# Weights of rounds 2 and 3 of an expert network read from a ring of three places that on-chip copies fill

## The reference

```python
cur = xn
for r in range(4):                      # R = 4 rounds
    logits = cur @ Wg[r] + bg[r]        # E = 4 experts
    vals, idx = top_k(logits, 2)
    cw = sum(one_hot(idx, 4) * softmax(vals))
    hmid = gelu(einsum('nh,ehf->enf', cur, W1) + b1)    # 128 -> 512, all four experts
    y = einsum('enf,efh->enh', hmid, W2) + b2           # 512 -> 128
    cur = cur + einsum('ne,enh->nh', cw, y)
```

## Time and profile before

| | us |
|---|---|
| median of 2 runs | 784.92 (784.88 to 784.97) |
| span of the profiled execution, first to last instruction | 782.9 |
| TensorE with matmuls in flight | 777.2 |
| VectorE busy | 689.3 |
| ScalarE busy | 641.1 |
| POOL busy | 115.2 |

### The profile page before, as it was taken

The page is one execution under the profiler, slowest core; times in us unless marked ns, Lnnn a source line. Parts: engine busy times, 40 slices in busy tenths (PEclk is TensorE's granted clock), DMA queues, the critical chain, the costliest instruction groups (busy, mean ns, idle before and its releaser), DMA issues.

```text
span 782.9 us, 9951 instructions
## 1 busy us (share of the span) xinstructions
PE 777.2 (99%) x3392; PEld 619.2 (79%) x3392; DVE 689.3 (88%) x1096; ACT 641.1 (82%) x873; POOL 115.2 (15%) x141
## 2 busy tenths in 40 slices
PE   8999999999999999999999999999999999999998
PEld 6778788887888878888788887888877788888887
DVE  7999987899888889879899788987988989988998
ACT  7989888787888877888788877887877878888886
POOL 0122111111111111111111111111111111111110
PEclk9999999999999999999999999999999999999999
DMA  8467572332642416333154322643227434655453
GB/s 267 139 132 182 128 208 50 95 95 41 148 89 62 107 28 163 92 64 88 33 157 107 81 57 41 149 108 96 41 41 175 108 56 107 134 123 122 70 117 71
DMA packets 77010, 81.62 MB, mean 104 GB/s; under 512 B 48800, under 2 KB 54688, under 8 KB 72992
## 3 DMA queue, kind: packets, MB, share of 16 engines
q0 software_dynamic: 18624, 34.61, 25.8%
q1 hardware_dynamic: 57920, 46.11, 19.5%
q10 hardware_dynamic: 416, 0.26, 0.1%
HBM read 41.91 MB, written 3.93 MB: 59 GB/s over the span
## 4 chain that ended last, share of the span: by engine, by line
PE 95%; ACT 2%; DVE 2%; issue 0%; DMA 0%; DVEq 0%
PE h_bank L1079 15%; PE h_bank L1080 15%; PE h_bank L1083 15%; PE y_bank L1152 15%; PE y_bank L1142 15%; PE y_bank L1140 14%; PE p_bank L1079 2%; PE p_bank L1083 2%; PE p_bank L1080 2%; PE r_bank L1189 1%; ACT g L465 1%; ACT g_hi L471 1%; DVE g_lo L759 0%; DMA cur<-in_x 0%; DVE stats L600 0%
## 5 line engine op out<-in xcount | busy, mean ns | idle before, releaser
L465 ACT ACTIVATE g<-h_bank,b_c 128x512 f32<-128x512 f32 x512 | 329.3, 682 | 77.8 <-PE h_bank L1083 77.0
L759 DVE TENSOR_TENSOR g_lo<-g,g_hi 128x1024 fp32r<-128x1024 f32 x256 | 310.0, 1222 | 72.8 <-ACT g_hi L471 71.2
L471 ACT ACTIVATE g_hi<-g 128x1024 fp32r<-128x1024 f32 x256 | 271.8, 1062 | 8.1
L415 POOL DMA_DIRECT2D cur<-tmp x126 | 110.6, 878 | 642.4 <-DVE tmp L773 544.1
L1079 PE MATMUL h_bank<-cur_hi,w_hi 128*128 128x512 f32 x512 | 202.9, 396 | 0.2 <-ACT cur_hi L513 0.2
L1083 PE MATMUL h_bank<-cur_lo,w_hi 128*128 128x512 f32 x512 | 202.2, 395 | 0.0
L1080 PE MATMUL h_bank<-cur_hi,w_lo 128*128 128x512 f32 x512 | 202.1, 395 | 0.0
L1140 PE MATMUL y_bank<-g_hi,w_hi 128*128 128x512 f32 x504 | 196.2, 393 | 0.0
L1142 PE MATMUL y_bank<-g_hi,w_lo 128*128 128x512 f32 x488 | 193.6, 397 | 0.0
L1152 PE MATMUL y_bank<-g_lo,w_hi 128*128 128x512 f32 x504 | 137.9, 395 | 0.1
L1079 PEld LDWEIGHTS h_bank<-cur_hi,w_hi 128*128 128x128 f32 x512 | 96.2, 188 | 26.6 <-issue 3.8
(11 more groups left out here) (153 smaller groups left out, 410.5 us busy)
## 6 DMA issues: line engine op xcount, KB each, us to landing
cur<-tmp POOLq DMA_DIRECT2D x126, 256.0 KB, 3.3
cw_b<-cw_scratch SPq DMA_DIRECT2D x31, 1024.0 KB, 5.2
xn_t<-cur SPq DMA_DIRECT2D x8, 256.0 KB, 3.1
cur<-in_x SPq DMA_DIRECT2D x7, 256.0 KB, 5.0
xr<-in_x SPq DMA_DIRECT2D x28, 64.0 KB, 3.4
out<-o SPq DMA_DIRECT2D x28, 64.0 KB, 2.1
xn_scratch<-o POOLq DMA_DIRECT2D x6, 256.0 KB, 3.0
xr<-xn_scratch SPq DMA_DIRECT2D x24, 64.0 KB, 2.5
```

Of the source, the lines that this page charges most:

```text
L415: pool.dma_start(cur[:, block_of(s // E)], tmp[:, s % SUMS, :], accum_op=ALU.add).then_inc(summed, DMA)
L465: nc.scalar.activation(g[:, gb, ft * BLK:(ft + 1) * BLK], hb[ft][:, :], ACT.Gelu_apprx_tanh, bias=b1_c[:, e * FT + ft:e * FT + ft + 1]).th ...
L471: nc.scalar.activation(g_hi[:, gb, h], g[:, gb, h], ACT.Copy).then_inc(g_hi_done, 1)
L759: nc.vector.tensor_tensor(g_lo[:, gb, h], g[:, gb, h], as_f32(g_hi[:, gb, h]), ALU.subtract).then_inc(g_lo_done, 1)
```

## The change

The high and low parts of an expert's weights now lie side by side, `w1_all[:, e]` and `w2_all[:, e]`, 4 KB per partition each; `w1_hi` and the others are views of them. A new tensor `staged` has three places of 4 KB per partition. In steps 32 to 95 up and down read their weights from places of `staged` instead. Each use of a weight set is a unit v, in the order in which TensorE wants them: w1(32), w1(33), w2(32), w1(34), w2(33), ..., w2(95), and unit v goes to place v % 3. SP fills a place with one DMA of 512 KB from `w1_all` or `w2_all`, after the product that read unit v-3 is done: w1(s+1) after down(s-2), w2(s) after up(s). The product waits for its unit (`stage_full`). The copies stand in SP's order ahead of `spread_gates(k)`: first those of the steps 4(k-1) to 4k-1, then the gates of turn k. The matmuls, their number and their data are as before.

Besides, `g` and `g_lo` now share one address range, so that line 759 writes `g_lo` over the `g` that it reads.

```diff
+STAGES, STAGED_FROM, STAGED_TO = 3, 32, 96
...
-        w1_hi, w1_lo = sb("w1_hi", [128, E, F], f32r), sb("w1_lo", [128, E, F], f32r)
-        w2_hi, w2_lo = sb("w2_hi", [128, E * FT, D], f32r), sb("w2_lo", [128, E * FT, D], f32r)
+        w1_all, w2_all = sb("w1_all", [128, E, 2, F], f32r), sb("w2_all", [128, E, 2, F], f32r)
+        w1_hi, w1_lo = w1_all[:, :, 0, :], w1_all[:, :, 1, :]
+        w2_hi, w2_lo = (w2_all[:, :, n, :].rearrange("p e (t d) -> p e t d", d=D) for n in range(2))
+
+        staged = sb("staged", [128, STAGES, 2, F], f32r)
...
-        g = sb("g", [128, 2, FT * BLK])
-        g_hi, g_lo = sb("g_hi", [128, 2, FT * BLK], f32r), sb("g_lo", [128, 2, FT * BLK], f32r)
+        g_hi = sb("g_hi", [128, 2, FT * BLK], f32r)
+        place = nc.sbuf_base
+        sb("g_place", [128, 2, FT * BLK])
+        g = nc.alloc_sbuf_tensor_at("g", [128, 2, FT * BLK], f32, offset=place)
+        g_lo = nc.alloc_sbuf_tensor_at("g_lo", [128, 2, FT * BLK], f32r, offset=place)
...
+        def unit_of_w1(s):
+            return 0 if s == STAGED_FROM else 2 * (s - STAGED_FROM) - 1
+
+        def unit_of_w2(s):
+            return 2 * (s - STAGED_FROM) + 2 if s < STAGED_TO - 1 else 2 * (s - STAGED_FROM) + 1
+
+        def w1_of(s):
+
+            if STAGED_FROM <= s < STAGED_TO:
+                q = unit_of_w1(s) % STAGES
+                return staged[:, q, 0, :], staged[:, q, 1, :]
+            return w1_hi[:, s % E, :], w1_lo[:, s % E, :]
...
+            def stage(v, src):
+
+                if v >= STAGES:
+                    u = v - STAGES
+                    n = STAGED_TO - STAGED_FROM
+                    if u == 2 * n - 1:
+                        sp.wait_ge(down_done, STAGED_TO)
+                    elif u == 0 or u % 2 == 1:
+                        sp.wait_ge(up_done, FT * (STAGED_FROM + (u + 1) // 2 + 1))
+                    else:
+                        sp.wait_ge(down_done, STAGED_FROM + (u - 2) // 2 + 1)
+                sp.dma_start(staged[:, v % STAGES, :, :].bitcast(f32), src.bitcast(f32)).then_inc(stage_full[v % STAGES], DMA)
+
+            def stage_step(s):
+
+                if s == STAGED_FROM:
+                    stage(unit_of_w1(s), w1_all[:, s % E, :, :])
+                if s + 1 < STAGED_TO:
+                    stage(unit_of_w1(s + 1), w1_all[:, (s + 1) % E, :, :])
+                stage(unit_of_w2(s), w2_all[:, s % E, :, :])
+
             END_TURN = END_FROM // E
             for k in range(4, END_TURN):
+                for s in range(E * (k - 1), E * k):
+                    if STAGED_FROM <= s < STAGED_TO:
+                        stage_step(s)
                 spread_gates(k)
...
+                w1h, w1l = w1_of(s1)
+                if STAGED_FROM <= s1 < STAGED_TO:
+                    v = unit_of_w1(s1)
+                    pe.wait_ge(stage_full[v % STAGES], DMA * (v // STAGES + 1))
...
-                    mm_high(hb[ft][:, :], w1_hi[:, e, w], w1_lo[:, e, w], cur_hi[:, q, :])
+                    mm_high(hb[ft][:, :], w1h[:, w], w1l[:, w], cur_hi[:, q, :])
...
+                w2h, w2l = w2_of(s)
+                if STAGED_FROM <= s < STAGED_TO:
+                    v = unit_of_w2(s)
+                    pe.wait_ge(stage_full[v % STAGES], DMA * (v // STAGES + 1))
```

More of the change, by code:

```diff
@@ L207, in mixer_gated_experts @@
         combined = sem("combined")
+        stage_full = [sem(f"stage_full{q}") for q in range(STAGES)]
         r_full, r_empty = sem("r_full"), sem("r_empty")
@@ L228, in as_f32, with as_f32r, w2_of @@
             return ap.bitcast(f32)
+        def as_f32r(ap):
+            return ap.bitcast(f32r)
+        def unit_of_w1(s):
[7 more added lines that the diff above has]
+            return w1_hi[:, s % E, :], w1_lo[:, s % E, :]
+        def w2_of(s):
+            if STAGED_FROM <= s < STAGED_TO:
+                q = unit_of_w2(s) % STAGES
+                return tuple(staged[:, q, n, :].rearrange("p (t d) -> p t d", d=D) for n in range(2))
+            return w2_hi[:, s % E, :, :], w2_lo[:, s % E, :, :]
         GATEW, SMALL, MIXW = 2, 3, 2
@@ L429, in high_w2 @@
                 act.wait_ge(w2_loaded[e], DMA)
-                nc.scalar.activation(w2_hi[:, e * FT:(e + 1) * FT, :], w2_raw[e], ACT.Copy).then_inc(w2_high, 1)
+                nc.scalar.activation(w2_hi[:, e, :, :], w2_raw[e], ACT.Copy).then_inc(w2_high, 1)
             def high_mixw():
@@ L639, in low_w2 @@
             def low_w2(e):
-                h = slice(e * FT, (e + 1) * FT)
                 dve.wait_ge(w2_high, e + 1)
-                nc.vector.tensor_tensor(w2_lo[:, h, :], w2_raw[e], as_f32(w2_hi[:, h, :]),
+                nc.vector.tensor_tensor(w2_lo[:, e, :, :], w2_raw[e], as_f32(w2_hi[:, e, :, :]),
                                         ALU.subtract).then_inc(w2_low, 1)
@@ L1139, in down @@
                     hi = g_hi[:, b, ft * BLK:(ft + 1) * BLK]
-                    nc.tensor.matmul(yb[b][:, :], w2_hi[:, e * FT + ft, :], hi, start=(ft == 0), stop=False)
+                    nc.tensor.matmul(yb[b][:, :], w2h[:, ft, :], hi, start=(ft == 0), stop=False)
                     if s >= E:
-                        nc.tensor.matmul(yb[b][:, :], w2_lo[:, e * FT + ft, :], hi, start=False, stop=False)
+                        nc.tensor.matmul(yb[b][:, :], w2l[:, ft, :], hi, start=False, stop=False)
                 if s < E:
@@ L1146, in down @@
                     for ft in range(FT):
-                        nc.tensor.matmul(yb[b][:, :], w2_lo[:, e * FT + ft, :], g_hi[:, b, ft * BLK:(ft + 1) * BLK],
+                        nc.tensor.matmul(yb[b][:, :], w2l[:, ft, :], g_hi[:, b, ft * BLK:(ft + 1) * BLK],
                                          start=False, stop=False)
@@ L1151, in down @@
                         pe.wait_ge(g_lo_done, 2 * s + ft // 2 + 1)
-                    last = nc.tensor.matmul(yb[b][:, :], w2_hi[:, e * FT + ft, :], g_lo[:, b, ft * BLK:(ft + 1) * BLK],
+                    last = nc.tensor.matmul(yb[b][:, :], w2h[:, ft, :], g_lo[:, b, ft * BLK:(ft + 1) * BLK],
                                             start=False, stop=(ft == FT - 1))
@@ L1168, in down_halves @@
                         hi = g_hi[:, b, ft * BLK + n * HALF:ft * BLK + (n + 1) * HALF]
-                        nc.tensor.matmul(sums[n][:, 0:HALF], w2_hi[:, e * FT + ft, :], hi, start=(ft == 0), stop=False)
-                        nc.tensor.matmul(sums[n][:, 0:HALF], w2_lo[:, e * FT + ft, :], hi, start=False, stop=False)
+                        nc.tensor.matmul(sums[n][:, 0:HALF], w2h[:, ft, :], hi, start=(ft == 0), stop=False)
+                        nc.tensor.matmul(sums[n][:, 0:HALF], w2l[:, ft, :], hi, start=False, stop=False)
                     for ft in range(FT):
@@ L1174, in down_halves @@
                         lo = g_lo[:, b, ft * BLK + n * HALF:ft * BLK + (n + 1) * HALF]
-                        last = nc.tensor.matmul(sums[n][:, 0:HALF], w2_hi[:, e * FT + ft, :], lo, start=False, stop=(ft == FT - 1))
+                        last = nc.tensor.matmul(sums[n][:, 0:HALF], w2h[:, ft, :], lo, start=False, stop=(ft == FT - 1))
                     last.then_inc(done, 1)
```

3 lines of the change are left out of this document (2 added, 1 removed).

## The result

The kernel takes 879.42 us with the change (875.87 to 882.98, 2 runs) against 784.92: the ratio is 1.121, 95% interval 1.110 to 1.131. The forecast was 826 us with a range of 793 to 868: the direction was right, the size too small by more than half. The profiled execution has a span of 881.1 us, 98.2 more than before.

A forecast was written before the change was run, and what follows sets the result against it. TensorE was taken as the bound, so waits add in full: 12 x 1.9 + 3 x 4.1 = 35.1 us plus 6 for accumulates, 41 us on the 784.92 us median, gave 826 us, range 793 to 868.

The forecast's parts named there:

- the sum of 41 us: Total added time: 35.1 us of waits at the ends of turns 9 to 23, plus 6 us for accumulates.
- What can be gained: nothing: All 64 staged steps: a weight's place does not set the matmul interval, so 0 us gained.
- g_lo over g: 0: VectorE's tensor_tensor, twice a step, now written in place: no new wait and no cost, 0 us.
- In an ordinary step I take 0: Copies in ordinary steps: each lands some 3.5 us after issue, within the 5.59 us step, so 0 us.
- Turns 9 to 23 are 15: Count of turns with a stall: 12 ordinary and 3 longer ones, 35.1 us together.
- Late by 1.7 us ... 1.9 us: Ordinary turn: copy of w1(4k+1) lands 1.7 us late behind store and broadcast; 1.9 with the first weight load.
- the list's own terms: Ordinary turn's timeline: store issued at 3.3, landed at 6.3; broadcast 5.4 us; copy 1.4 us later, at 13.2.
- I take 0.4: Accumulates falling into a turn's store, broadcast and copy: 0.4 us a turn, 6 us over 15 turns.
- a way to be wrong in size: Closing caveat: the size fails if accumulates beside the copy cost more than 0.4 us a turn.
- late by 3.9 us, 4.1 with the load: Turns 12, 16, 20: gates made late, so copy of w1(4k+1) is 3.9 us late, 4.1 with weight load.
- rival 3: Clock falls to 1.2 GHz at each of 15 waits, 2.8 us more each: 42 us more, 868 us; chance 0.04.
- the long ones alone: Clock falls only at the three long waits: 8 us more, 834 us; chance 0.05, within the turns' stall.

The follow-up runs named there:

- e2: The changed kernel with all 128 copies still issued, but up and down read weights at home and wait for no copy: 784.89 us, ratio 0.9997.
- e3: The changed kernel with the gates' broadcast of turns 8 to 23 cut to 16 of 2048 columns: 806.51 us, ratio 1.028.
- e7: On top of e4, SP's order alone changed, the gates' store and broadcast placed between the copies: 814.71 us, ratio 1.036.
- e1: The changed kernel with no copies and no reads from the ring, only the weight layout and g_lo over g kept: 784.5 us, ratio 0.9996.
- e4: The changed kernel with the first three copies issued ahead of the gates of turn 8: 865.94 us, ratio 1.104.
- e12: On top of e4, accumulates of steps 4k-3 and 4k-2 in turns 9 to 23 add 16 of 512 columns: 842.96 us, ratio 1.074.
- e11: On top of e4, POOL's queue issues the gates' store and broadcast of turns 9 to 23, SP's holds copies alone: 825.14 us, ratio 1.052.

## Why the prediction was wrong

Three terms of the sum failed, and the sum of 41 us became 97. Turn 8 had no term (11.5 us of waiting), the lateness of a turn was too small (61.8 us in fifteen turns where 41 were put), and the clock after a wait was put at nothing (24 us).

The mechanism of the waits was right, and where it was placed too: the wait stands before up(4k+1), once a turn, behind the gates' store and broadcast on SP's queue; in turns 9 to 23 it is longest at turns 12, 16 and 20; nothing happens at the other products or outside rounds 2 and 3; the interval of the matmuls at full clock is still 0.23 us; the DMA engines do have room. e2 shows that it is the wait and not the traffic, e3 and e7 that it is the broadcast and what else stands ahead of the copy. Point by point:

- *"What can be gained: nothing"*, *"g_lo over g: 0"*: right (e1, 0.9996).
- *"In an ordinary step I take 0"*: right, no wait outside the turns' ends. A copy lands in 2.9 us at the least, I had put 3.5 for one alone.
- *"Turns 9 to 23 are 15"*: wrong. There are 16 waits. The sum has no term for the first three copies. They wait for no product, but they stand behind spread_gates(8) in SP's order, and turn 8 is the first of a batch like 12, 16 and 20. That is 11.5 us of waiting, and 13.5 us of time by e4.
- *"Late by 1.7 us ... 1.9 us"* for ordinary turns: 3.6 us in the mean of the twelve. By the list's own terms (means of these turns), the store landed after 3.5 us (put 3.0), the broadcast after 6.4 (put 5.4), the copy behind it 1.9 us later (put 1.4). Without the two accumulates (e12) it is 1.9 us, the number put, but that is luck: the broadcast takes 0.9 us more than put, and the store 0.4 less, the copy behind the broadcast 0.1 less, and the 0.19 us for the weight load doesn't show (the first matmul starts 0.04 us after the landing).
- *"I take 0.4"* for accumulates: mis-sized, 1.3 us in an ordinary turn (e4 less e12), which the prediction had named as a way to be wrong in size. With both the twelve ordinary turns lose 42.7 us where I had 27.6.
- Turns 12, 16, 20, *"late by 3.9 us, 4.1 with the load"* and 0.4 for accumulates, 13.5 in all: 19.1 us. At turn 12 the store's place was right (4.05 us before the end of down(47), 4.21 in the rows; 3.9 and 3.3 at turns 16 and 20), but broadcast and copy took 9.1 us instead of 6.8: store at 327.76, broadcast one landing later, first matmul at 338.23. About half of the difference stood in the trace of before. I took the median of all broadcasts for turn 12, whose own had landed after 6.5 us, with an accumulate beside it:

```profile
L321 SPq DMA_DIRECT2D cw_b<-cw_scratch x1: 337/337/337, 298.0 to 298.0; - x1
...
DMA to landing us min/median/max: 6.5/6.5/6.5
```

- *The clock* stood in rival 3, with 0.04 in full and nothing in the sum: 24 us of slow matmuls, in 72 us at 1.2 GHz. Waits alone, 73 us, would have given 858, inside the range. But the time is 11 us over the range's upper end of 868, so turn 8 costs the range just as well: without its wait it is 866 (e4). Rival 3 had the right kind of number (2.8 us for a wait; 24 us over 16 waits are 1.5), and I gave it 0.04, and 0.05 for the long ones alone, because the only rows at hand had no wait in them. A case that no row prices needs a chance, not the lowest one.

The three misses add up: 41 us put, and 11.5 for turn 8, 21 for the size of the fifteen waits (61.8 less 41), 24 for the clock: 97 of the 98.2 us of span.

What stays open: why the broadcast lands 1.1 us later in the median with the copies around it. Small accumulates don't shorten it (e12, 6.4), and copies aren't needed for such a time: in e1, where none runs, those of turns 12 and 16 landed after 6.5 us and that of turn 20 after 6.3. Whether the copies or the moments of its issue do it wasn't tried. What sets the clock's fall after one wait and not after another is open as well.

## What to carry to other kernels

Before a transfer is put on a queue on which other transfers stand with waits of their own, walk through every place of the queue's order, the first round included, and ask what stands before the copy that is needed next: here 64 MB of copies that nobody waited for were free (0.9997), and waiting for them behind one store, its landing and one broadcast cost 12%, the clock included. Give a ring at least as much slack as the longest transfer that can come between two of its copies; the first copies ahead of the gates, a better order and a fourth place took 84 of 94 us back. And price a wait of the matmul engine at its length and what the clock does after it, here a third on top.

## What the runs showed of the hardware

- After a wait TensorE's clock was granted at 1.2 GHz for a stretch, with matmuls 0.43 us apart, and this did not depend on the wait's length alone: in e4 an interval of 2.61 us between two matmuls (from 284.62 us) was followed by slow ones and one of 3.03 us (from 228.56) wasn't. Matmuls put into the wait, with no use for their results, kept the clock up (0.994 against 0.961) and made the kernel faster by 14 us.
- A copy of 512 KB from on-chip memory to on-chip memory, 4 KB a row, landed in 2.9 us at the best and 4.0 in the median. 64 MB of them beside a core at full work, at 0.86 of the DMA engines' time, left the busy time of TensorE (391.0 us), VectorE (338.2 against 338.3) and ScalarE (317.2 against 317.3) in rounds 2 and 3 as it was (e2); what they lengthened were other DMAs (an accumulate landed after 3.6 us in the median, from 3.3), with no cost in time.
- A broadcast of 1 MB on another queue than the copies made them late as well (e11): copies alone on their queue landed 6.6 to 9.8 us after their issue when a broadcast from the other queue was in flight, against 4.1 in the median. A queue of its own did not give a transfer its own time on the engines.
